# Three rounded products for the scores, column tiles for states and their use, and remade lists

## What is computed

```python
x = x + attention(layernorm(x), Wq, Wk, Wv, Wo)
x = x + experts(layernorm(x), gate_w, bias, Wg, Wu, Wd, Wg_s, Wu_s, Wd_s)
```

```python
kv_sum += outer(k_i, v_i); k_sum += k_i
out_i = (q_i @ kv_sum) / (q_i . k_sum + 1e-8)
```

## Time and profile before

| what | value |
|---|---|
| median of three runs | 1030.51 us |
| profiled execution, its own time | 1031.95 us |
| its span in the profile | 1030.2 us |
| matmul, busy | 1007.4 us |
| weight load, busy | 859.6 us |
| VectorE, busy | 838.3 us |
| GpSimd, busy | 537.6 us |
| ScalarE, busy | 422.3 us |
| mean granted clock of TensorE | 0.998 |

### The profile page before, as it was taken

How to read it: one execution, slowest core, us unless ns; L and a number is a source line. 1 busy time by engine, 2 the same in 40 slices (tenths; PEclk the granted TensorE clock), 3 DMA queues, 4 the chain that set the end, 5 groups by cost and what they waited for, 6 DMA issues and landing times.

```text
span 1030.2 us, 22106 instructions
## 1 busy us (share of the span) xinstructions
PE 1007.4 (98%) x8437; PEld 859.6 (83%) x8437; DVE 838.3 (81%) x1776; ACT 422.3 (41%) x750; POOL 537.6 (52%) x440
## 2 busy tenths in 40 slices
PE   6889999999999999999999999999999999999997
PEld 5768888888888888888888888888888888888886
DVE  4888888888978889898788978889888888977554
ACT  5754343434434344343434434344343434422222
POOL 5864545556354463545556345463545556343643
PEclk9999999999999999999999999999999999999999
DMA  5011425345252543425345253444424345231321
GB/s 204 3 47 57 104 63 137 66 117 110 62 144 60 137 83 105 109 58 139 67 114 111 59 142 70 135 83 104 107 64 136 66 121 114 59 107 58 102 82 42
DMA packets 235160, 96.48 MB, mean 94 GB/s; under 512 B 161712, under 2 KB 217520, under 8 KB 235056
## 3 DMA queue, kind: packets, MB, share of 16 engines
q1 hardware_dynamic: 235056, 95.07, 36.1%
...
## 4 chain that ended last, share of the span: by engine, by line
PE 90%; DVE 3%; ACT 2%; DMA 2%; issue 1%; POOL 1%; SPq 0%; DVEq 0%; ACTq 0%; POOLq 0%
PE bank L997 55%; PE y_bank L997 19%; PE bank L1106 6%; PE bank L1122 5%; PE bank L1093 2%; PE bank L1136 2%; PE bank L1148 1%; DMA cw_all<-in_w_qkvo 1%; DMA x_dram<-blocks 0%; DMA cw_all<-cw_dram 0%; DMA expo<-x_dram 0%; ACT wg_hi L580 0%; DVE et L965 0%; DVE x_mid L990 0%; ACT expo L641 0%
## 5 line engine op out<-in xcount | busy, mean ns | idle before, releaser
L997 PE MATMUL bank<-xt_hi,wg_hi 128*128 128x512 f32 x576 | 237.4, 412 | 3.0 <-DVE et L965 2.3
L746 POOL TENSOR_TENSOR h_lo<-et,h_hi 128x512 fp32r<-128x512 f32 x142 | 180.9, 1290 | 96.6 <-ACT h_hi L696 96.4
L997 PE MATMUL bank<-xt_lo,wg_hi 128*128 128x512 f32 x576 | 228.5, 397 | 0.0
L997 PE MATMUL bank<-xt_hi,wg_lo 128*128 128x512 f32 x576 | 228.5, 397 | 0.0
L743 POOL TENSOR_TENSOR et<-et,cw_all 128x512 f32<-128x512 f32 x124 | 163.5, 1339 | 115.1 <-DVE et L971 97.6
L871 DVE TENSOR_TENSOR scores<-bank,cst 128x512 f32<-128x512 f32 x240 | 152.6, 681 | 41.4 <-PE bank L1106 34.1
L997 PE MATMUL y_bank<-wd_hi,h_hi 128*128 128x256 f32 x576 | 165.0, 286 | 0.3 <-POOL h_lo L746 0.3
L997 PE MATMUL y_bank<-wd_hi,h_lo 128*128 128x256 f32 x576 | 161.5, 280 | 0.0
L997 PE MATMUL y_bank<-wd_lo,h_hi 128*128 128x256 f32 x576 | 161.4, 280 | 0.0
L997 PEld LDWEIGHTS bank<-xt_hi,wg_hi 128*128 128x128 f32 x576 | 108.6, 189 | 40.5 <-issue 16.8
L965 DVE SCALAR_TENSOR_TENSOR et<-et,bank 128x512 f32<-128x512 f32 x144 | 95.9, 677 | 48.7 <-ACT et L687 48.6
...
## 6 DMA issues: line engine op xcount, KB each, us to landing
...
x_dram<-blocks SPq DMA_DIRECT2D x112, 128.0 KB, 3.3
...
```

Source lines behind the costliest of these rows:

```text
L746: nc.gpsimd.tensor_tensor(h_lo[:, i % HR, :], et[:, i % ET, :], h_hi[:, i % HR, :].bitcast(f32), ALU.subtract).then_inc(h_lo_done, 1)
L997: ins = nc.tensor.matmul(dst, l, r, start=first and n == 0, stop=last and n == 2, skip_group_check=shared)
```

## The change

- `scores` from batch 2 on: the operands are `k_hi`, `k_lo`, `q_hi` and `q_lo` (fp32r). Per chunk three matmuls for each of the four row tiles are added up: k_hi*q_hi, k_hi*q_lo, k_lo*q_hi. Batches 0 and 1 keep the two float32 operands. `q_half` now lies in the memory of `blocks`.
- New parts: `k_split` on ScalarE (k_hi) and on GpSimd (k_lo), and `q_split` on VectorE (q_lo, two instructions per half). ScalarE's `q_split` writes `q_hi` in place of `q_half`. `scores` waits for k_lo and q_lo.
- `state`: for each chunk four matmuls in column tiles, each with 32 columns of k as weights and 32 columns of v moving. Only the 32x32 blocks on the diagonal are computed. VectorE's mask reads these blocks four times over by a broadcast, its output is as large as before.
- `inter`: for each chunk four matmuls in column tiles, each with 32 columns of the state as weights and 128 tokens moving.
- Start: constants have a semaphore of their own. Bias and router weights are loaded in a new part `small`, later in SP's list, and the router waits for them. The masks of batch 0 wait for single pieces of the weights.
- `XB` is 3; x is loaded one step earlier. The scratch memory for dynamic DMAs is set to 512.
- The lists of all engines and the table `BANK` are new.

The core of the diff:

```diff
-ET, HR, CW, SM, XB = 3, 3, 4, 8, 2
+ET, HR, CW, SM, XB = 3, 3, 4, 8, 3
 STEP = { "PE":
-        up.5.3 wo.1.2 wo.0.2 down.0.3 down.1.3 scores.1.1 gate.6.3 down.2.3 gate.8.3 up.8.3 gate.7.3 up.7.3
-        up.6.3 down.3.3 state.1.1 down.4.3 scores.2.1 values.0.1 values.1.1 down.5.3 inter.0.1 inter.1.1
-        scores.3.1 gate.0.2 router.0.2 values.2.1 values.3.1 gate.1.2 up.0.2 inter.2.1 inter.3.1 gate.2.2
-        k.0.0 q.0.0 k.1.0 up.2.2 down.6.3 up.1.2 q.1.0 down.7.3 down.8.3 scores.0.0 up.4.2 v.1.0 v.0.0
-        gate.4.2 gate.5.2 state.0.0 gate.3.2 up.3.2
+        up.5.3 wo.1.2 wo.0.2 down.0.3 scores.1.1 down.2.3 down.1.3 gate.7.3 gate.8.3 gate.6.3 up.6.3 up.8.3
+        down.3.3 up.7.3 state.1.1 values.0.1 values.1.1 scores.2.1 down.4.3 down.5.3 scores.3.1 gate.0.2
+        inter.0.1 router.0.2 values.2.1 inter.1.1 inter.2.1 values.3.1 inter.3.1 gate.1.2 up.0.2 gate.2.2
+        down.6.3 k.0.0 q.0.0 up.2.2 k.1.0 up.1.2 q.1.0 v.0.0 down.7.3 down.8.3 scores.0.0 up.3.2 v.1.0
+        gate.4.2 up.4.2 gate.3.2 gate.5.2 state.0.0
 STEP = { "DVE":
...
+        gate.6.3 up.8.3 up.6.3 state.1.1 blocks.0.0 mask.9.1 up.7.3 mask.11.1 mask.10.1 mask.8.1 mask.14.1
+        mask.12.1 mask.13.1 mask.15.1 spread.1.1 router.0.2 spread.0.1 route.0.2 mult.1.1 gate.0.2 mult.0.1
+        gate.1.2 up.0.2 gate.2.2 rank0.0.2 k.0.0 rank1.0.2 q.0.0 cum.0.0 up.2.2 k.1.0 cum.1.0 blocks.2.0
+        q_split.0.0 up.1.2 q.1.0 result.0.3 mask.0.0 mask.3.0 den.0.0 mask.1.0 mask.2.0 at.1.1 den.1.0
+        gate.4.2 at.0.1 gate.3.2 state.0.0 gate.5.2 up.4.2 up.5.2 wo.1.1 up.3.2 wo.0.1 ln2_stats.0.1
+        mask.4.0 mask.7.0 ln2_apply.0.1 blocks.1.1 mask.5.0 mask.6.0 ln1_stats.0.-1 q_split.1.0 gate.8.2
+        gate.7.2
...
+                elif name == "k_split":      # ScalarE
+                    act.wait_ge(drained[BANK["k", i]], USES["k", i, b])
+                    nc.scalar.activation(k_hi[:, i, :], kf[:, i, :], ACT.Copy).then_inc(k_hi_done, 1)
+                elif name == "k_split":      # GpSimd
+                    nc.gpsimd.tensor_tensor(k_lo[:, i, :], kf[:, i, :], k_hi[:, i, :].bitcast(f32), ALU.subtract)
+                elif name == "q_split":      # VectorE
+                    dve.wait_ge(q_half_done, Q_HALF["q_split", i, b])
+                    for j in range(2):
+                        last = nc.vector.scalar_tensor_tensor(q_lo[:, j, :], qf[:, i, :], cst[:, C_EO + j:C_EO + j + 1],
+                                                              q_hi[:, j, :].bitcast(f32), ALU.mult, ALU.subtract)
                     for c in range(SUBS - 1):           # state
-                        last = nc.tensor.matmul(bk[:, c * P:(c + 1) * P].rearrange("p (g t d) -> p g t d", t=2, d=DH),
-                                                k_tok[:, i, c, :], v_win[:, c, i * 4:(i + 1) * 4, 0:3:2, :],
+                        for g in range(4):
+                            rows = slice(32 * g, 32 * g + 32)
+                            last = nc.tensor.matmul(
+                                bk[rows, c * 2 * DH:(c + 1) * 2 * DH].rearrange("p (t d) -> p t d", d=DH),
+                                k_tok[:, i, c, rows], v_win[:, c, i * 4 + g, 0:3:2, :],
+                    if ("k_split", m, b) in K_LO:       # scores
+                        pe.wait_ge(k_lo_done, K_LO["k_split", m, b])
+                        pe.wait_ge(q_lo_done, Q_LO["q_split", m, b])
+                        pairs = ((k_hi, q_hi[:, :, :]), (k_hi, q_lo[:, :, :]), (k_lo, q_hi[:, :, :]))
+                        for n, (keys, queries) in enumerate(pairs):
+                            for g in range(4):
+                                last = nc.tensor.matmul(
...
+                                    keys[rows, m, cs], queries[rows, :, cs],
+                                    start=n == 0, stop=n == len(pairs) - 1)
-                        last = nc.tensor.matmul(bank[BANK["o", m]][:, c * P:(c + 1) * P], st[:, m, c - 1, :],
-                                                qf[:, m, c * P:(c + 1) * P], start=False, stop=True,
+                        for g in range(4):              # inter
+                            rows = slice(32 * g, 32 * g + 32)
+                            last = nc.tensor.matmul(bank[BANK["o", m]][rows, c * P:(c + 1) * P], st[:, m, c - 1, rows],
+                                                    qf[:, m, c * P:(c + 1) * P], start=False, stop=True,
```

More of the change, by code:

```diff
@@ L51 @@
+        split.0.2 split.1.2 split.2.2 weigh.4.2 weigh.5.2 weigh.3.2 rstd2.0.1
         """,
     "DVE": """
[L53 to L56 removed]
@@ L72 @@
[L72 to L74 removed]
+        turn.1.0 turn.0.0 warm.8.0 k.0.0 q.0.0 k.1.0 v.0.0 v.1.0 q.1.0 scores.0.0 k_turn.0.0 warm.17.0
+        scores.1.0 turn.1.1 k_turn.1.0 turn.0.1 values.0.0 state.0.0 scores.2.0 values.1.0 scores.3.0 k.0.1
+        q.0.1 inter.0.0 inter.1.0 state.1.0 values.2.0 values.3.0 inter.2.0 inter.3.0 scores.0.1 q.1.1 k.1.1
@@ L75 @@
+        wo.1.0 wo.0.0 scores.1.1 k_turn.1.1 v.1.1 k_turn.0.1 v.0.1 state.0.1 values.0.1 scores.2.1 inter.1.1
+        turn.2.0 turn.3.0 warm.10.0 inter.0.1 values.1.1 state.1.1 scores.3.1 gate.0.0 gate.1.0 turn.0.2
+        turn.1.2 router.0.0 gate.2.0 k.0.2 values.2.1 values.3.1 inter.3.1 inter.2.1 q.0.2 up.0.0 v.1.2
+        up.1.0 k.1.2 q.1.2 k_turn.0.2 v.0.2 scores.0.2 up.2.0 state.0.2 gate.3.0 gate.4.0 up.4.0 gate.5.0
+        up.3.0 k_turn.1.2
         """,
     "ACT": """
-        piece.0.0 piece.1.0 turn.1.0 turn.0.0 piece.2.0 v.1.0 piece.3.0 k.0.0 piece.4.0 piece.5.0 q.0.0 k.1.0
@@ L102 @@
+        den.1.2 up.4.0 gate.5.0 up.3.0 state.0.2 up.5.0 wo.0.1 wo.1.1 ln2_stats.0.1 mask.4.2 mask.5.2
+        ln2_apply.0.1 blocks.1.1 mask.7.2 mask.6.2 ln1_stats.0.3 gate.8.0 q_split.1.2 gate.7.0
         """,
     "SP": """
-        load_x.0.0 consts.0.0 piece.0.0 piece.1.0 piece.2.0 load_x.0.1 piece.3.0 piece.4.0 piece.5.0 piece.6.0
-        piece.7.0 load_x.0.2 piece.8.0 piece.9.0 cw_store.0.0 cw_load.3.0 cw_load.0.0 cw_load.2.0 cw_load.1.0
-        cw_load.5.0 cw_load.4.0 cw_load.7.0 cw_load.6.0
+        load_x.0.0 consts.0.0 piece.0.0 piece.1.0 piece.3.0 piece.2.0 load_x.0.1 piece.5.0 piece.9.0
@@ L107 @@
+        piece.4.0 piece.6.0 load_x.0.2 piece.7.0 small.0.0 piece.8.0 cw_store.0.0 cw_load.0.0 cw_load.1.0
+        cw_load.2.0 cw_load.4.0 load_x.0.3 cw_load.3.0
         """,
@@ L110 @@
     "PE": """
-        up.5.13 wo.0.14 wo.1.14 scores.1.15 down.0.13 gate.6.13 down.1.13 gate.7.13 gate.8.13 down.2.13
-        up.6.13 up.8.13 state.1.15 down.3.13 down.4.13 values.0.15 values.1.15 up.7.13 scores.2.15 down.5.13
-        gate.0.14 scores.3.15 down.6.13 router.0.14 down.7.13 inter.0.15 gate.1.14 inter.1.15 values.2.15
-        values.3.15 down.8.13 up.0.14 inter.2.15 inter.3.15 gate.2.14 gate.3.14 up.1.14 up.2.14 wo.0.15
-        wo.1.15 down.0.14 up.4.14 gate.7.14 up.3.14 gate.4.14 gate.5.14 up.6.14 down.1.14 up.5.14 down.2.14
@@ new lines @@
+        up.6.13 down.5.13 up.8.13 down.3.13 state.1.15 values.0.15 values.1.15 inter.1.15 scores.2.15
+        up.7.13 down.4.13 gate.0.14 scores.3.15 down.6.13 router.0.14 gate.1.14 up.0.14 down.7.13 gate.2.14
+        down.8.13 values.2.15 inter.0.15 inter.2.15 inter.3.15 values.3.15 gate.3.14 up.1.14 up.2.14 wo.0.15
+        wo.1.15 gate.5.14 gate.7.14 gate.4.14 up.3.14 down.0.14 up.4.14 up.5.14 down.1.14 gate.8.14
+        gate.6.14 down.2.14 up.8.14 down.3.14 up.6.14 up.7.14 down.4.14 router.0.15 gate.0.15 up.0.15
@@ L139 @@
-        mask.6.15 up.6.13 state.1.15 gate.8.13 up.8.13 gate.7.13 up.7.13 mask.8.15 mask.9.15 mask.11.15
-        mask.10.15 mask.12.15 mask.13.15 mask.15.15 spread.1.15 router.0.14 spread.0.15 gate.0.14 mask.14.15
-        route.0.14 rank0.0.14 rank1.0.14 up.0.14 result.0.13 mult.1.15 mult.0.15 gate.2.14 at.1.15 gate.1.14
-        gate.3.14 at.0.15 up.1.14 up.2.14 wo.1.15 wo.0.15 ln2_stats.0.15 up.3.14 ln2_apply.0.15 blocks.1.15
-        gate.4.14 gate.5.14 up.4.14 up.5.14 gate.6.14 up.6.14 gate.8.14 gate.7.14 up.8.14 up.7.14 router.0.15
@@ L284, in linear_attention_moe @@
         landed = [t[:, :, :].rearrange("p h (a k n) -> p (h a) k n", k=KC, n=P) for t in (expo, num_t)]
-        q_half = sb("q_half", [P, 2, S])
+        k_hi, k_lo = (sb(f"k_{n}", [P, KC, S], f32r) for n in ("hi", "lo"))
+        q_hi, q_lo = (sb(f"q_{n}", [P, 2, S], f32r) for n in ("hi", "lo"))
         blocks = sb("blocks", [P, SUBS * D])
+        q_half = blocks[:, :].rearrange("p (j n) -> p j n", j=2)
         k_tok = sb("k_tok", [P, KC, SUBS - 1, P])
@@ L425, in wait_blocks @@
                 wait_for(eng, put_done, 64 * n)
+            else:
+                for j in range(4):
+                    wait_filled(eng, "scores", j, UNSPLIT - 1)
         def wait_weighed(eng, i, b):
```

219 lines of the change are left out of this document (115 added, 104 removed).

## The result

The changed kernel took 1011.89 us (median of 4 runs, 1010.61 to 1011.97), the kernel before 1030.49 us in the runs beside it (1029.66 to 1031.1): ratio 0.9817, 95% interval 0.98 to 0.9834. That is 18.6 us less; 1014.6 was forecast, with 1004 to 1028 as the range. The profiled execution has a span of 1010.2 us, 20.0 less than before, where the sum gave 15.9.

The account below looks back on a forecast made before the run. TensorE's own work was taken to set the time. Scores -8.7, state -11.8, inter -0.3, shape changes +3.4, waits +2 and start -0.5 summed to -15.9 on the 1030.2 us span; forecast median 1014.6 us, range 1004 to 1028.

Parts of the forecast that it names:

- a column trip: Changing from full array to column tiles and back, as around values or the lone state.0.0: 0.32 us each.
- What bounds the kernel: In the 13 steps TensorE's own work sets the time; a us taken out of each step is worth 13 us.
- Scores: Six rounds of rounded matmuls at 0.117 us replace four at 0.215 per part: -8.7 us, bounds -11.8 and +24.
- rival (4): In scores, rounded row tiles stay at 0.215 us a round: +24 for -8.7, 1047 us; chance 0.10 shared with late q_lo.
- State: Six rounds of 32 columns take 0.30 us a part in place of 0.67: -11.8 us, bounds -16.3 and -0.3.
- Rival (1): Small state records cost by count, 29 ns each, 0.70 us a part: +1.0 for -11.8, total 1027.4 us; chance 0.19.
- Waits for q_lo: PE waits at scores.0.0 for VectorE's q_lo: +2 us charged over the run, 0 to +6 in the range.
- 1.7 us to spare: Ahead of scores.0.0, VectorE's 5.3 us of work fits within PE's 7 us of parts, leaving this slack.
- the 5.3: VectorE's needed time in us before scores.0.0: relu and exp 1.2, k 0.6, scan 1.2, blocks 1.0, q_lo 1.3.
- Room on VectorE: Four q_lo instructions add 2.7 us per batch: VectorE busy from 53.9 of 62 to 56.6 of about 61 us.
- Start, x and order: Earlier first weight pieces give -0.5 us; the third x buffer 0; the remade order 0, +-4.
- Rival (2): Lists gain more: state at 0.16 and 5 us of idle at both ends, 1005 us; chance 0.11.

Follow-up runs that it names:

- state put back: Changed kernel with state alone as before, one full-array matmul per chunk: 1019.31 us, ratio 0.9869 to the kernel before.
- inter put back: Changed kernel with inter alone as before, one full-array matmul per chunk: 1016.1 us, ratio 0.9841 to the kernel before.
- lists alone: Changed kernel with scores, state and inter all computed as before; lists, third x buffer and start remain: 1027.36 us, ratio 0.9956 to the kernel before.

## Why the prediction was right

The mechanism, the bound and the sign were right, and the sum was 4.1 us short of the span's fall. That it came so close in the steps is in part luck: the waits cost more than was charged, and PE's own work fell by a little more too. By its own steps:

| term | predicted | measured | by |
|---|---|---|---|
| a scores part | -0.156 | -0.166 | timelines |
| a state part | 0.30 | 0.33 alone; 0.40 to the values | timelines |
| state with its added trip, per step | 2 x -0.37 + 0.33 = -0.41 | -0.50; -0.46 in the shortest steps | state put back |
| a column trip | 0.32 | 0.34; 0.31 in the shortest steps | inter put back |
| waits in 13 steps | +2 | +3.5 (4.42 less 0.95 before) | gaps of PE |
| lists, in the steps | 0 beside the trip more | +0.07 each, less than one profile varies; +0.30 in the shortest steps, the trip | lists alone |
| 13 steps in all | -11.7 | -12.6 | periods |
| outside of them | -4.2 | -7.4 | the table above |

The -11.7 is the sum without one batch of scores (0.6), three of state (2.2), the 0.9 of trips and the 0.5 of the start, which lie outside. The 0.9 is a slip: three changes of shape are one and a half trips, 0.5 us, so the whole sum should have been 15.5. In the shortest steps the sum without waits, -1.05 a step, is to be held against 61.55 to 60.41, -1.14. What lies above the shortest step rose from 0.24 to 0.42 a step.

- *What bounds the kernel*: right. What was taken from PE's work in a step arrived in the time, less the new waits.
- *Scores*: right to 0.01 a part. Rounded row tiles come 0.12 apart, as full-array ones; rival (4) is refuted.
- *State*: right within its bounds. Rival (1), 29 ns for each record, is refuted: 8 ns. The rule of 60 cycles for each matmul, by the section "Instruction Overhead" of the Trainium skill's page "TensorEngine Tiling (Array Packing)", would make 24 records an estimated 0.60 us if they added up one behind the other; the trace shows 0.20 between the first start and the last, so they don't. A round of four starts 0.03 us behind the one before it, near the 0.027 by width. Small records in column tiles don't cost by their count here.
- *Waits for q_lo*: the place was right (`scores.0.0`), the size too low and the mechanism incomplete. The step that failed is "1.7 us to spare"; the runs show 0.58. It took 0.677 for each q_lo from line 965, whose second operand lies in PSUM. With both operands in SBUF and GpSimd at work, one of the two takes 1.77. The at_lo of the kernel before, min 681 and max 1840, had shown this. And the wait that ends last is the one for bank 1, behind q_lo: the evaluation that frees it, 0.6 us more of VectorE, is missing from the 5.3. That the median still came out near is no merit of this term.
- *Room on VectorE*: 56.6 of 61 was forecast, 55.31 measured. The rise was right (2.7 forecast, 52.75 to 55.35 as means of 13 steps measured), the window that it started from was one of the fuller ones. But the load told nothing of room at one place: q_lo done twice, with VectorE busy for 58 of 62.3 us, made the undisturbed steps 1.9 us longer and cost 3.0 with the clock.
- *Start, x and order*: the sum gave 0 for the order, and here most of the missing 4.1 lies. At the end the lists gained 4.4, by one store that no longer stands ahead of a load, and the clock's fall that came with the gap in this profile. The earlier trace rows had shown both (5.9 idle, clock 0.96), and the text took the tail for "a chain of last results and a store". Rival (2), which let the lists gain 5 us at both ends, had that part right. At the start the changed kernel is 1.3 us later at the first Wo. It has new gaps of PE of 1.25 and 1.39 us (at 29.4 and 32.2), and then 3.4 us at half the clock. But neither can be called the cause: the 11 kernels with the new start (some with small edits in it) have these two gaps, and they reach the first Wo between 50.12 and 53.23 us, where the three with the old lists need 50.18 to 50.48. With inter put back it is 50.12, although its clock is at half for 6.8 us, and with state put back 52.14, although its clock stays at 1.00. So the new start is later in most profiles, the clock doesn't decide it, and the cause stays open.
